# A pair recurrence whose feed-forward part moves one slot back, with new queue orders on four engines

## The reference, cut to what matters

```python
xa = _ln(x, ln1_w, ln1_b)
sx = concatenate([state[:, 1:2] - xa[:, :1], xa[:, :-1] - xa[:, 1:]], axis=1)
xxx = einsum('blfd,fde->blfe', tanh((xa + sx * maa_x) @ maa_w1).reshape(b, l, 5, DM), maa_w2)
xk, xw, xv, xr, xg = unstack(xa[:, :, None] + sx[:, :, None] * (maa_stack + xxx))
w = exp(-exp(time_decay + tanh(xw @ td_w1) @ td_w2))
r, k, v, g = xr @ Wr.T, xk @ Wk.T, xv @ Wv.T, silu(xg @ Wg.T)
# for each t: a = k_t v_t ; out = r_t . (u * a + s) ; s = a + w_t * s
og = group_norm(out) * gn_w + gn_b
x1 = x + og * g @ Wo.T
xc = _ln(x1, ln2_w, ln2_b)
sx2 = concatenate([state[:, 0:1] - xc[:, :1], xc[:, :-1] - xc[:, 1:]], axis=1)
rr = sigmoid((xc + sx2 * ffn_maa_r) @ Wfr.T)
kk = square(relu((xc + sx2 * ffn_maa_k) @ Wfk.T))
return x1 + rr * (kk @ Wfv.T)
```

## Time and profile before

| what | before |
|---|---|
| median of 3 runs | 2133.93 us (2133.77 to 2134.12) |
| the profiled execution's own time | 2134.8 us |
| its span, first to last instruction | 2133.1 us |
| mean granted TensorE clock | 0.957 |
| busy, whole span: TensorE, VectorE, ScalarE, POOL | 91%, 60%, 50%, 24% |
| the recurrence | from about 1765 us to the end |

### The profile page before, as it was taken

One profiled execution on the slowest core, in us unless ns is written; L12 is line 12 of the kernel. 1 busy time (PEld: TensorE's weight loads), 2 busy tenths in 40 slices (PEclk: granted clock), 3 DMA queues, 4 the chain that ended last, 5 costly groups with the idle time before them and its releaser, 6 DMA issues. The chain is left out here.

```text
span 2133.1 us, 40585 instructions
## 1 busy us (share of the span) xinstructions
PE 1937.6 (91%) x15496; PEld 1698.7 (80%) x15496; DVE 1279.9 (60%) x2546; ACT 1076.3 (50%) x2920; POOL 511.7 (24%) x346
## 2 busy tenths in 40 slices
PE   6999996998999999999899999999988986899874
PEld 4677774997999999999689999999988984566653
DVE  6888886235555555555555555555552364888873
ACT  3787877544444334443453344434346543566653
POOL 3555453543200000000240000000005514223220
PEclk9999999999999999999999999999998997899986
DMA  5000001300000000002200000000030000000000
GB/s 189 2 2 2 2 2 42 118 1 6 6 6 5 0 5 5 5 5 89 75 6 1 6 5 5 5 0 5 28 91 1 1 1 1 1 11 6 10 7 10
DMA packets 29533, 40.72 MB, mean 19 GB/s; under 512 B 1922, under 2 KB 21476, under 8 KB 29156
## 3 DMA queue, kind: packets, MB, share of 16 engines
q1 hardware_dynamic: 29412, 39.06, 5.5%
HBM read 32.76 MB, written 2.10 MB: 16 GB/s over the span
## 5 line engine op out<-in xcount | busy, mean ns | idle before, releaser
L762 DVE TENSOR_TENSOR w_head_lo<-banks,w_head_hi 128x512 fp32r<-128x512 f32 x128 | 88.0, 691 | 252.5 <-ACT w_head_hi L674 244.9
L693 ACT ACTIVATE arena<-banks 128x512 f32<-128x512 f32 x128 | 69.5, 593 | 298.1 <-PE banks L551 298.1
L470 POOL TENSOR_TENSOR w_hT_lo<-arena,w_hT_hi 128x512 fp32r<-128x512 f32 x16 | 20.6, 1290 | 813.1 <-ACT w_hT_hi L648 813.1
L686 ACT ACTIVATE arena<-banks,arena 128x129 f32<-128x129 f32 x512 | 180.6, 374 | 40.1 <-DVE arena L742 40.0
L960 POOL TENSOR_TENSOR arena<-arena 128x1024 f32<-128x1024 f32 x64 | 150.7, 2378 | 161.9 <-DVE arena L1246 161.9
L674 ACT ACTIVATE w_head_hi<-banks 128x512 fp32r<-128x512 f32 x128 | 76.1, 597 | 191.6 <-PE banks L561 191.6
L1164 ACT ACTIVATE arena<-arena 128x128 f32<-128x128 f32 x512 | 162.6, 394 | 1.8 <-DVE arena L1255 1.7
L116 PE MATMUL banks<-w_kv_lo,w_hi 128*128 128x256 f32 x512 | 147.1, 287 | 9.9 <-DVE arena L728 9.9
L116 PE MATMUL banks<-w_wo_lo,w_head_hi 128*128 128x256 f32 x512 | 148.6, 290 | 1.3 <-DVE w_head_lo L762 1.3
L118 PE MATMUL banks<-w_kv_hi,w_hi 128*128 128x256 f32 x512 | 147.0, 287 | 0.0
L117 PE MATMUL banks<-w_kv_hi,w_lo 128*128 128x256 f32 x512 | 146.9, 287 | 0.0
(11 more groups left out here) (299 smaller groups left out, 5696.4 us busy)
## 6 DMA issues: line engine op xcount, KB each, us to landing
arena<-in_L_xattn_wq SPq DMA_DIRECT2D x8, 512.0 KB, 4.8
arena<-in_L_xattn_wk SPq DMA_DIRECT2D x8, 512.0 KB, 5.8
arena<-in_L_xattn_wv SPq DMA_DIRECT2D x8, 512.0 KB, 6.6
arena<-in_L_xattn_wo SPq DMA_DIRECT2D x8, 512.0 KB, 9.4
arena<-ctx_t SPq DMA_DIRECT2D x16, 256.0 KB, 2.5
x<-in_x SPq DMA_DIRECT2D x4, 512.0 KB, 6.5
ctx_t<-in_ctx_t SPq DMA_DIRECT2D x1, 2048.0 KB, 11.7
arena<-in_L_xattn_w SPq DMA_DIRECT2D x2, 1024.0 KB, 12.8
```

The source lines that it names most:

```text
L686: done = act.activation(prob[:, b, i, :], score_tile(c, j), ACT.Exp, scale=SCALE, bias=shift[:, b, i:i + 1], accum_out=total[:, b, i:i + 1])
L693: act.activation(probT[:, b, :, :], bank[5 + b][:, :].rearrange("p (h q) -> p h q", h=HG), ACT.Copy).then_inc(probT_ok, 1)
L762: dve.tensor_tensor(head_lo[:, two, :], bank[5 + half][:, :].rearrange("p (h t) -> p h t", h=2), head_hi[:, two, :], ALU.subtract).then_in ...
```

## The change

The feed-forward part moves from pair p - 1 to pair d = p - 2, and there is one slot more at the end (p runs to NP + 1). group norm, gate, output projection and residual stay at c = p - 1. Beyond that:

- times_gate and multiply_rk go from POOL to VectorE. POOL is left with the five adds in a row and finish.
- The mixes use only banks X and Y (Z before), and the first two of pair p + 2 are made at the end of slot p, ahead of centre and variance; the first two of pair 0 in slot -1. tanh_low is made a slot earlier too.
- TensorE: spread_v(p, 1) goes ahead of project_v, and of project_out; project_out ahead of project_r; a_transpose directly behind c_transpose; spread_v(p + 1, 0) ahead of project_ff; a_low ahead of bonus_sums; sum_heads(p, 3) behind them.
- VectorE: shift_a goes ahead of the fourth unit, the gate between the second unit's scan and times_r, the residual into the third unit.
- ScalarE: normalise2 goes ahead of group_rstd; row_rstd behind sigmoid_rr and ahead of tanh_low and copy_raw.
- In the last slots another order, with the keys' product of the last but one pair in bank Y.

The diff, without the slots of VectorE and ScalarE that repeat the pattern:

```diff
-        MIX = [X, Y, Z, X, Y]
+        MIX = [Y, X, Y, X, Y]
+        def kk_bank(c):
+            return Y if c == NP - 2 else Z
-            for p in range(-1, NP + 1):
+            for p in range(-1, NP + 2):
...
@@ block.gpsimd @@
             def slot(p):
-                u, a, c = exists(p), exists(p + 1), exists(p - 1)
-                if a:
-                    add_xa(p + 1, range(0, FR))
-                if c:
-                    times_gate(p - 1)
-                if a:
-                    add_xa(p + 1, range(FR, F))
-                    multiply_rk(p + 1)
-                if c:
-                    finish(p - 1)
+                if exists(p + 1):
+                    add_xa(p + 1, range(0, F))
+                if exists(p - 2):
+                    finish(p - 2)
...
             def a_transpose(a):
-                wait(pe, read["xc"], a - 2)
+                wait(pe, read["xc"], a - 3)
-            def a_mix(a):
+            def a_mix(a, fs):
                 pe.wait_ge(read["low"], a + 1)
-                for f in range(F):
-                    if f == 0:
+                for f in fs:
+                    if f == 1:
                         wait(pe, read["c"], a)
-                    elif f == 2:
-                        wait(pe, read["var"], a - 1)
-                    elif f > 2:
-                        pe.wait_ge(f_read, a * F + (f - 2))
+                    elif f > 1:
+                        pe.wait_ge(f_read, a * F + (f - 1))
             def low_rate(a):
-                pe.wait_ge(f_read, a * F + 3)
+                wait(pe, read["var"], a - 1)
...
@@ block.tensor @@
             def slot(p):
                 if a:
-                    a_mix(p + 1)
+                    if p + 1 == 0:
+                        a_mix(0, (0, 1))
+                    a_mix(p + 1, range(2, F))
                     low_rate(p + 1)
                     project_k(p + 1)
+                if p == NP:
+                    c_transpose(p - 2)
+                    project_kk(p - 2)
+                if u:
+                    spread_v(p, 1)
+                if a:
                     project_v(p + 1)
+                if u:
+                    sum_heads(p, 0)
+                if a:
+                    project_rate(p + 1)
                 if c:
                     project_out(p - 1)
-                if u:
-                    sum_heads(p, 0)
-                    spread_v(p, 1)
                 if a:
-                    project_rate(p + 1)
                     project_r(p + 1)
                 if u:
                     sum_heads(p, 1)
                 if a:
                     project_g(p + 1)
-                if c:
-                    c_transpose(p - 1)
+                if d and p != NP:
+                    c_transpose(p - 2)
+                if exists(p + 2):
+                    a_transpose(p + 2)
                 if u:
                     sum_heads(p, 2)
-                if c:
-                    project_kk(p - 1)
-                    project_rr(p - 1)
-                if exists(p + 2):
-                    a_transpose(p + 2)
-                if c:
-                    project_ff(p - 1)
-                if u:
-                    sum_heads(p, 3)
+                if d:
+                    if p != NP:
+                        project_kk(p - 2)
+                    project_rr(p - 2)
                 if a:
                     spread_v(p + 1, 0)
+                if d:
+                    project_ff(p - 2)
+                if exists(p + 2):
+                    a_low(p + 2)
+                if a:
                     bonus_sums(p + 1)
                 if u:
+                    sum_heads(p, 3)
+                if exists(p + 2):
+                    a_mix(p + 2, (0, 1))
+                if u:
                     centre(p)
-                if exists(p + 2):
-                    a_low(p + 2)
-                if u:
                     variance(p)
```

More of the change, by code:

```diff
@@ L1886, in _ @@
             gp.wait_ge(made, 13)
[L1888 to L1892, removed]
             def add_xa(a, fs):
@@ L1898, in add_xa @@
                     gp.tensor_tensor(to, to, xa[:, :, :, 1:P + 1], ALU.add).then_inc(mix_ok, 1)
[L1900 to L1904, removed]
             def finish(c):
@@ L2055, in bonus_sums @@
                 pe.wait_ge(read["g"], a + 1)
-                wait(pe, read["rr"], a - 1)
+                wait(pe, read["rr"], a - 2)
                 for k in range(KC):
@@ L2069, in variance @@
                 wait(pe, read["td"], min(p + 2, NP))
-                wait(pe, read["ff"], p)
+                wait(pe, read["ff"], p - 1)
                 pe.matmul(Z[:, :], mean_w[:, :], square[:, :], start=True, stop=True).then_inc(ready["var"], 1)
@@ L2079, in c_transpose @@
                 pe.wait_ge(xn2_ok, c * PAIR + PAIR)
-                pe.wait_ge(read["r"], min(c + 3, NP))
+                pe.wait_ge(read["r"], min(c + 4, NP))
                 wait(pe, read["xc"], c)
@@ L2085, in project_kk @@
                 pe.wait_ge(xk_ok, c * (2 * KC) + KC)
-                pe.wait_ge(read["out"], c + 1)
-                feature_major(Z, w["Wfk"], xk2).then_inc(ready["kk"], 1)
+                if c == NP - 2:
+                    pe.wait_ge(read["xc"], c + 1)
+                else:
+                    pe.wait_ge(read["out"], min(c + 2, NP))
+                if c == NP - 1:
+                    pe.wait_ge(read["ff"], c)
+                feature_major(kk_bank(c), w["Wfk"], xk2).then_inc(ready["kk"], 1)
             def project_rr(c):
                 pe.wait_ge(xk_ok, c * (2 * KC) + 2 * KC)
-                pe.wait_ge(read["g"], min(c + 3, NP))
-                pe.wait_ge(read["c"], min(c + 2, NP))
+                pe.wait_ge(read["g"], min(c + 4, NP))
+                pe.wait_ge(read["c"], min(c + 3, NP))
+                wait(pe, read["rr"], c)
                 token_major(X, xr2, w["Wfr"]).then_inc(ready["rr"], 1)
@@ L2271, in slot @@
             def slot(p):
-                u, a, c = exists(p), exists(p + 1), exists(p - 1)
+                u, a, c, d = exists(p), exists(p + 1), exists(p - 1), exists(p - 2)
                 if c:
                     square_centred(p - 1)
-                if a:
-                    tanh_low(p + 1)
+                if d:
+                    normalise2(p - 2)
                 if c:
                     group_rstd(p - 1)
+                if d and p == NP:
+                    copy_xc(p - 2)
                 if u:
@@ L2294, in slot @@
                     copy_r(p + 1)
-                if c:
-                    normalise2(p - 1)
+                if exists(p + 2):
+                    normalise(p + 2)
                 if a:
                     tanh_g(p + 1)
-                if c:
-                    copy_xc(p - 1)
+                if d and p != NP:
+                    copy_xc(p - 2)
                 if a:
@@ L2303, in slot @@
                 if exists(p + 2):
[L2304 to L2307, removed]
+                    copy_xa(p + 2)
+                if d:
+                    square_relu(p - 2)
+                if c and p == NP:
+                    row_rstd(p - 1)
+                if d:
+                    sigmoid_rr(p - 2)
+                if c and p != NP:
+                    row_rstd(p - 1)
                 if exists(p + 2):
-                    copy_xa(p + 2)
+                    tanh_low(p + 2)
                 if u:
@@ L2322, in _ @@
             copy_xa(0)
+            tanh_low(0)
             slots(slot)
@@ L2423, in gate_ff, with multiply_rk, times_gate @@
                 dve.tensor_tensor(gated[:, :, :], halves(Z), r_gate[:, :, :], ALU.mult).then_inc(read["ff"], 1)
+            def multiply_rk(a):
+                dve.wait_ge(read["r"], a + 1)
+                dve.wait_ge(read["k"], a + 1)
+                wait(dve, ready["c"], a)
+                dve.tensor_tensor(rk[:, :, :], rT[:, parity(a), :, :], kT[:, parity(a), :, :], ALU.mult).then_inc(rk_ok, 1)
+            def times_gate(c):
+                dve.wait_ge(affine_ok, c + 1)
+                dve.wait_ge(read["g"], c + 1)
+                wait(dve, ready["out"], c)
+                dve.tensor_tensor(zT[:, :, :], affine[:, :, :], gate[:, parity(c), :, :], ALU.mult).then_inc(z_ok, 1)
             def unit(p, s):
@@ L2434, in slot @@
                     make_bonus(p)
+                if d:
+                    row_shift(p - 2)
+                if u:
                     scan(p, 0)
@@ L2440, in slot @@
                     unit_variance(p - 1)
+                if d and p == NP:
+                    shift_c(p - 2)
                 if u:
-                    unit(p, 1)
+                    weigh_keys(p, 1)
+                    scan(p, 1)
+                if c:
+                    times_gate(p - 1)
+                if u:
+                    times_r(p, 1)
+                    weigh_keys(p, 2)
+                    scan(p, 2)
                 if c:
@@ L2445, in slot @@
                 if u:
-                    weigh_keys(p, 2)
```

(17 more changed lines are left out.)

10 lines of the change are left out of this document (5 added, 5 removed).

## The result

| | before | after |
|---|---|---|
| median of 7 runs | 2133.87 us (2132.64 to 2134.51) | 2143.83 us (2137.25 to 2144.68) |
| ratio | | 1.0040, 95% interval 1.0029 to 1.0052 |
| profiled execution: own time, span | 2134.8, 2133.1 us | 2137.25, 2135.5 us |
| first mix to first mix, slots 2 to 5, together | 148.8 us | 146.8 us |

Slower by 0.4%, where 0.7% faster was forecast, and outside the range. The profiled execution is the fastest of the seven, so its profile shows 2.4 us of the 10; the rest is taken up at the end of the experiments.

The account below looks back on a forecast made before the run. Neither TensorE nor VectorE bound the last stage; they take turns. 1842.5 + 33.0 + 4 x 34.5 + 33.3 + 3.0 = 2049.8, plus drain 68.9 = 2118.7, + 1.7 - 0.9 = 2119.5 us; range 2107 to 2132.

Parts of the forecast that it names:

- slots 2 to 5: Four full slots of the last stage, forecast at 34.5 us each before an allowance for half clock.
- M2: Time when VectorE begins to mix pair 2: 1842.5 us forecast, between 1841.0 (full clock) and 1844.5 (half clock).
- slot 1: Slot without feed-forward: VectorE to its end at 31.9 us, plus 1.1 for half clock, 33.0.
- slot 6: Slot without a_transpose, a_low or shift_a: 33.3 us to the end of times_r.
- drain: From the end of slot 6 to the end of the span: 68.9 us against 66.5 before, bounds 66.5 and 73.
- the steady slot: Walk of a clean full slot from td at 3.33 us to the next slot's start at 34.5, against 36.14.
- M: Moment when VectorE begins to mix a pair; slots are cut there and times within a slot count from it.
- the wait for z: TensorE's wait before Wo, up to 1.3 us in four of six slots; forecast to go, Wg ending 1.2 sooner.
- The first slots: Slots -1 to 1: M1 stays at 1808.4, M2 at 1842.5 (-0.6), slot 1 takes 33.0 us.
- The clock: Half clock costs 0.6 us a slot, chosen between 0 and 1.1; 3.0 over slots 2 to 6.
- slower: the clock: Rival: more TensorE waits drop slots 2 to 6 to clock 0.75, losing 4.7 us each; 2140, chance 0.10.
- The slot stays: Rival: reordered queues lose their saving in the slot's tail, slots 2 to 6 keep 37.2 us; median 2131.2, chance 0.14.

Follow-up runs that it names:

- e1_two_banks: Kernel before with only the five mixes moved to banks Y, X, Y, X, Y instead of X, Y, Z, X, Y: 2138.98 us, ratio 1.0029.
- e2_lag_alone: Kernel before with only the feed-forward part (normalise2 to finish) moved to pair p - 2 and one slot more at the end: 2136.85 us, ratio 1.0018.
- e3_product_first: Changed kernel with the fourth product put ahead of shift_a on VectorE: 2131.31 us, ratio 0.9999 to the kernel before.
- e4_filled_wait: Changed kernel with 32 more matmul instructions, result never read, ahead of the spread in slots 0 and 1: 2133.77 us, ratio 0.9999 to the kernel before.
- e8: Changed kernel with one 384-column matmul added per slot between centre and variance: 2141.43 us, ratio 1.0046 to the kernel before.
- e9: Same added matmul, in the changed kernel with c_transpose (pairs 0 to 4) in bank Z and shift_c and fourth product earlier: 2122.04 us, ratio 0.9957.
- a2_changed: The changed kernel unaltered, second of three more looks for a profile near its median: 2142.12 us.

## Why the prediction was wrong

The account, by its own terms, against the profiled execution (us):

| term | forecast | profile | more by |
|---|---|---|---|
| M2 | 1842.5 | 1845.9 | 3.4 |
| slot 1 | 33.0 | 37.1 | 4.1 |
| slots 2 to 5 | 4 x 34.5 + 2.4 for the clock = 140.4 | 146.8 | 6.4 |
| slot 6 | 33.3 + 0.6 | 36.1 | 2.2 |
| drain | 68.9 | 69.6 | 0.7 |
| span | 2118.7 | 2135.5 | 16.8 |

The median is 24.3 above the forecast: these 16.8, the 6.6 between profiled execution and median, and the 0.9 that I had taken off for the opposite difference.

**The step that failed first** is the opening line of the steady slot, "L2023 (td) starts at 3.33". I carried it over from the trace of before, as if the adds on POOL alone set it, and priced the mixes' move to two banks at nothing. The walk of the slot's end had variance over at 35.1, 0.6 after the next M (1.38 measured), and never went on from there to td. What stood in this place before isn't in the earlier trace rows:

```profile
1879.56 1.14 PE L2016 MATMUL banks<-arena 32*128 32x256 f32 x8
...
1881.30 2.26 PE L2016 MATMUL banks<-arena 32*128 32x256 f32 x12 [0.60 <-ACT arena L2229]
```

Variance was over ahead of the first two mixes, the third began at 0.58, and the fifth had to wait only until the second was read, some 1.7 after M. All mixes were done at 2.84, and td waited 0.49 more for POOL. In the changed kernel variance stands behind M, the third mix begins at 1.38, VectorE reads it from 2.54 on, and the fifth, in the same bank, waits for this and begins at 3.47. td is 1.2 late in a clean slot. In e1_two_banks, where variance keeps its place, it is 0.75 late; the other 0.45 fits variance's new place, but no run takes this back alone.

What the delay costs a slot is arithmetic, not an experiment: behind td each stretch came out within 0.4 of the forecast, and the clean slot is 1.0 longer (35.46 for 34.5), which is 3.8 of the 6.4 over slots 2 to 5. Slot 6 has td at 4.5 too, so about 1.2 of its 2.2. Before, the wait for z behind td would have covered such a delay (e1_two_banks, e2_lag_alone). The forecast booked the end of this wait as a gain of 1.2 a slot, and didn't see that it had been the cover for what comes ahead of it.

**The second** is in "The first slots", and it is the larger: slots 0 and 1 are 7.5 of the 16.8. The wait of the spread was seen (4.5 us of idle TensorE in slot 1), but "so I add 1.1 for half clock" rests on no row. The trace of before had one: in its slot 0 the spread took 2.09 instead of 1.15 near a wait of 2.78. The two groups behind the new wait are spread and a_low, 1.07 and 1.94 from start to start, so some 3.0 more if both run at half the speed; 0.95 and 1.80 more were measured. The range for M2 had held this case ("1844.5"), but I chose 1842.5, and 1845.9 came. With the wait cut short (e3_product_first) or filled (e4_filled_wait) slots 0 and 1 took 34.0 and 33.1, or 34.1 and 32.7, where the forecast had 34.1 and 33.0. So this step accounts for all of the 7.5, though td is late in these slots as well (4.6 in slot 1). By the ratios of the runs it is worth 8 us.

**The clock** in slots 2 to 5: 0.6 a slot assumed, from "The longest new wait is 1.2, but there are more of them", and 1.24 found, no less than before (1.1). That shorter waits mean less half clock was an assumption, and e8 and e9 don't bear it out for the one place that they filled. What a phase of half clock costs also depends on the waits behind it: 0.07 in the slot of e2_lag_alone, 1.65 here. The rival "slower: the clock" had the number nearest to the median (2140), but its condition, 0.75 in slots 2 to 6, didn't come about: they show 0.95, and 0.87 at the lowest in a2_changed.

What held: from td to the end of Wg 13.6 us (13.8 forecast); the wait for z gone; the new wait of a_transpose 1.35 (1.2); from Wfk to the end of bonus_sums 9.6 (9.4); from there to the next M 4.3 (4.4); VectorE below the bound; all four times_r at 1.2; the drain 69.6 (68.9). The scans took 2.31 each, and the "up to 3.0" of one of them didn't come, as the adds on POOL ended 0.3 us before it began. row_rstd and its table loads cost nothing: in the clean slot the Exp behind the second load (1985.59, 1.28 long) began at 1986.88, and tanh_low at 1987.55, released by TensorE (the drain of 1.38 us that the Trainium skill, "ScalarE: Activation LUTs", What ACT_TABLE_LOAD costs, adds to a switch isn't there in this trace either). Because nearly all the errors were in the same direction, they added up.

"The slot stays" was the rival nearest in kind: slots 2 to 6 took 182.9 us where it had 186.0. Its 2131.2 was 12.6 below the median all the same: 7.5 for the too short slots 0 and 1, which it kept, 0.7 for the drain and 7.5 between profile and median, less the 3.1 by which its slots 2 to 6 were too long.

## What to carry to other kernels

When a queue is put in another order, write down everything that the engine does between the event from which time is counted and the first operation of the sum; a start time taken over from the old trace hides exactly what the change alters. When a bank is given to other work, ask for each wait which reading it now stands behind: here the fifth mix went from the second reading to the third. Before a wait is booked as a gain, see what it covered, for delays ahead of it count in full once it is gone. And where TensorE waits several microseconds, price what stands behind the wait at double its length; moving the awaited operation a place forward on the other engine, or filling the wait, were worth 8 us here, about what the whole change had cost.

## What the runs showed of the hardware that was not expected

- Four matmul instructions of one mix, which reads 32 of the 128 rows, took 1.12 us when alone (changed kernel, 1960.77); eight of two mixes on different rows took 1.14 (kernel before, 1879.56), so those two overlapped.
- After a TensorE wait of 4.67 us, spread and a_low took 2.09 and 3.81 us; with the wait filled, 1.15 and 2.11. The granted clock had fallen during the wait, 1.2 us ahead of its end.
- A phase of half clock of some 3.4 us (1888.3 to 1891.7 in the slot from 1883.06) lengthens a slot of the changed kernel by 1.65 us, and most full slots have one that begins 4.4 to 5.4 us after M, although TensorE's waits there are 0.6 and 0.7. Filling one of them changed nothing. In e2_lag_alone such a phase, ahead of a wait of 1.3, lengthened the slot by 0.07.
- The same kernel took from 2134.3 to 2144.7 us over its runs, in a schedule whose clean slots never differ by more than 0.1.
